# The last block of a large store as fifteen stores of two to fifteen partitions

## The reference

```
keep   = (u >= 0.1)
x_drop = x * keep / 0.9
h      = x + adj @ x_drop
out    = (h - mean(h)) / sqrt(var(h) + 1e-5)      # over the 64 columns of each row
```

## Time and profile before

| what | value |
|---|---|
| median of 3 runs (lowest to highest) | 641.73 us (641.69 to 641.83) |
| the profiled execution's own time | 641.88 us |
| its span, first to last instruction | 640.1 us |
| DMA over the span | 429 GB/s, 274.84 MB |
| TensorE matmul busy | 502.8 us (79%) |
| VectorE, ScalarE busy | 53.7 us, 17.7 us |
| large store (1984 KB), issue and landing | 626.82, 12.7 us later |
| last store (64 KB), issue and landing | 638.09, 1.6 us later |

### The profile page before, as it was taken

The page is one execution under the profiler, slowest core; times in us unless marked ns, Lnnn a source line. Parts: engine busy times, 40 slices in busy tenths (PEclk is TensorE's granted clock), DMA queues, the critical chain, the costliest instruction groups (busy, mean ns, idle before and its releaser), DMA issues.

```text
span 640.1 us, 5097 instructions
## 1 busy us (share of the span) xinstructions
PE 502.8 (79%) x2312; PEld 179.7 (28%) x2312; DVE 53.7 (8%) x102; ACT 17.7 (3%) x41; POOL 1.6 (0%) x14
## 2 busy tenths in 40 slices
PE   0097969688799578879878689867869868689997
PEld 0062213232233222223222223222323223133344
DVE  1930001010010100101000010100101001010101
ACT  0001000000000000000000000000000000000000
POOL 1000000000000000000000000000000000000000
PEclk9997979988799978889979899978999969799999
DMA  9999999999999999999999999999999999999998
GB/s 393 459 394 455 431 420 454 405 446 439 422 421 436 435 451 422 438 408 444 459 418 434 442 412 455 420 434 446 426 418 426 446 451 422 438 405 438 425 425 364
DMA packets 7207, 274.84 MB, mean 429 GB/s; under 512 B 800, under 2 KB 928, under 8 KB 1312
## 3 DMA queue, kind: packets, MB, share of 16 engines
q1 hardware_dynamic: 7056, 272.63, 98.8%
q10 hardware_dynamic: 144, 2.10, 0.8%
HBM read 272.63 MB, written 2.10 MB: 429 GB/s over the span
## 4 chain that ended last, share of the span: by engine, by line
DMA 62%; PE 33%; DVE 3%; another core or an unknown queue 1%; issue 0%; ACT 0%; SPq 0%; DVEq 0%; ACTq 0%
DMA ring<-adj 56%; PE acc L202 33%; DMA ring<-adj_last 5%; DMA xdrop<-u 2%; DVE node_sum L317 1%; DVE xdrop L321 1%; DVE xdrop L329 1%; PE folded L210 0%; DVE x_sb L321 0%; PE lifted L237 0%; SPq L126 0%; ACT squares L303 0%; PE lifted L263 0%; ACT std L308 0%
## 5 line engine op out<-in xcount | busy, mean ns | idle before, releaser
L202 PE MATMUL acc<-ring,xdrop 128*64 128x512 f32 (+1 forms) x2176 | 485.6, 606 | 103.1 <-DMA ring<-adj 101.7
L202 PEld LDWEIGHTS acc<-ring,xdrop 128*64 128x64 f32 x2176 | 162.8, 146 | 413.0 <-issue 280.2
L344 DVE SCALAR_TENSOR_TENSOR y<-folded,x_sb 128x256 f32<-128x256 f32 (+1 forms) x16 | 6.7, 416 | 552.3 <-PE folded L210 552.3
L237 PE MATMUL lifted<-x_sb,lift 128*128 128x64 f32 x4 | 1.1, 428 | 30.6 <-DVE x_sb L321 30.6
L210 PEld LDWEIGHTS folded<-fold,sums_T 128*128 128x128 f32 x128 | 15.5, 191 | 12.6 <-issue 12.6
L284 ACT COPY sums_T<-acc 128x512 f32<-128x512 f32 x15 | 8.8, 585 | 335.0 <-PE acc L202 335.0
L210 PE MATMUL folded<-fold,sums_T 128*128 128x64 f32 x128 | 17.7, 281 | 0.0
L277 ACT ACTIVATE std<-square_sum,eps 128x4 f32<-128x4 f32 (+1 forms) x16 | 4.8, 297 | 225.2 <-DVE square_sum L351 225.2
L237 PEld LDWEIGHTS lifted<-x_sb,lift 128*128 128x128 f32 x4 | 0.9, 322 | 30.5 <-issue 30.5
L348 DVE TENSOR_TENSOR squares<-y 128x256 f32<-128x256 f32 (+1 forms) x16 | 6.7, 417 | 0.5
L355 DVE TENSOR_TENSOR x_sb<-y,rstd 128x256 f32 (+1 forms) x16 | 6.7, 416 | 0.6
(11 more groups left out here) (23 smaller groups left out, 5.5 us busy)
## 6 DMA issues: line engine op xcount, KB each, us to landing
ring<-adj SPq DMA_DIRECT2D x13, 4096.0 KB, 31.3
ring<-adj SPq DMA_DIRECT2D x2, 2048.0 KB, 28.7
xdrop<-u ACTq DMA_DIRECT2D x1, 2048.0 KB, 12.5
x_sb<-x SPq DMA_DIRECT2D x1, 2048.0 KB, 12.3
out<-x_sb SPq DMA_DIRECT2D x1, 1984.0 KB, 12.7
ring<-adj_last SPq DMA_DIRECT2D x1, 1920.0 KB, 29.5
ring<-adj_last SPq DMA_DIRECT2D x1, 1792.0 KB, 33.4
ring<-adj_last SPq DMA_DIRECT2D x1, 1536.0 KB, 30.6
```

The source lines that it names most:

```text
L202: last = nc.tensor.matmul(acc[i][D * h:D * h + D, 0:cols], xdrop[:, k, :], piece[:, b, :], start=(k < 2), stop=(k >= NB - 2))
L344: nc.vector.scalar_tensor_tensor(out=y[:, 0:nj, :], in0=folded[:, 0:nj, :], scalar=1.0 / KEEP, in1=x_sb[:, bass.ds(block0, nj), :], op0=AL ...
```

## The change

The large store goes out with 61 blocks instead of 62. Behind it, with no wait between, SyncE issues 15 stores of the 62nd block: the first 9 partitions, then 15, 14, 13 and so on down to 2, which makes 128. Each has a semaphore of its own, and SyncE waits for each of them after the wait for the other two stores.

```diff
+GROUPS = (9, 15, 14, 13, 12, 11, 10, 9, 8, 7, 6, 5, 4, 3, 2)
...
+        groups = [(sum(GROUPS[:n]), size) for n, size in enumerate(GROUPS)]
...
+        group_stored = [sem(f"group_stored{n}") for n in range(len(groups))]
...
             sp.wait_ge(rows_ready, FINAL)
-            sp.dma_start(out[:, 0:NB - LAST_J, :], x_sb[:, 0:NB - LAST_J, :]).then_inc(stored, 16)
+            bulk = NB - LAST_J - 1
+            sp.dma_start(out[:, 0:bulk, :], x_sb[:, 0:bulk, :]).then_inc(stored, 16)
+
+            for n, (p0, size) in enumerate(groups):
+                sp.dma_start(out[p0:p0 + size, bulk:bulk + 1, :],
+                             x_sb[p0:p0 + size, bulk:bulk + 1, :]).then_inc(group_stored[n], 16)
             sp.wait_ge(rows_ready, FINAL + 1)
             sp.dma_start(out[:, NB - LAST_J:NB, :], x_sb[:, NB - LAST_J:NB, :]).then_inc(stored, 16)
             sp.wait_ge(stored, 32)
+            for n in range(len(groups)):
+                sp.wait_ge(group_stored[n], 16)
```

## The result

The changed kernel takes 644.24 us (median of 6 runs, 644.20 to 644.40) against 641.83 (6 runs, 641.69 to 642.00) of the kernel before: ratio 1.0038, 95% interval 1.0026 to 1.0049. It is slower by 2.4 us, four and a half times the 0.53 that was forecast, and above the range. The profiled execution took 644.23 with a span of 642.4, so the 1.8 around the span is unchanged and the whole difference lies in the span.

A forecast was written before the change was run, and what follows sets the result against it. The DMA stream of adjacency blocks sets the time up to a short tail. Only the waits counted: profiled 641.88 + 0.53 = 642.41, less 0.15 for the median, 642.26, stated as 642.25; range 641.6 to 643.1.

The forecast's parts named there:

- (a): Large store in the tail: losing one block shortens its rows, worth 0 to -0.05 us, taken as 0.
- (b): SyncE's issue of 15 small stores behind the large one: 7.4 us, done at 634.2, covered, no stall.
- (c): Small stores' rows and completions on the DMA rings: delay the last store by 0 to 0.7 us, taken as 0.
- Each completion holds its ring: Rival, DMA rings: each small store's completion blocks its ring 0.4 us, 15 in a row 6.0; time 646 to 648; chance 0.04.
- (d): SyncE's end: 15 more waits, paired into 7 or 8 instructions after the last store's landing, add 0.53 us.
- (e): 15 more semaphores: nothing in the span handles semaphores one by one, so 0.
- SyncE is held in issuing: Rival, SyncE's queue: slow or blocked small-store issues delay the last store; time 646.4 or 647; chance 0.05.
- A low ring is late: Rival, DMA tail: the busiest engine is among the seven late ones, adding 0.1 to 0.7 us; 642.4 to 643.0; chance 0.15.

The follow-up runs named there:

- the small loads: Changed kernel with one semaphore, the large store back at 62 blocks, and 15 same-shaped loads from HBM into spare SBUF replacing the small stores: 644.10 us, +2.28 over the kernel before.

## Why the prediction was wrong

**(a) The shorter large store: right.** It was counted at 0. The last store's packets go out at 638.9 in both kernels.

**(b) The issues: right, and too dear.** 5.45 for fifteen instead of 7.0, since a store of fewer than 16 partitions costs less: 403 ns for the first, 253 for the last, of two partitions. Neither the ring's room nor a count of transfers held SyncE.

**(c) The packets on the rings: this is the step that failed.** It priced a completion as a packet of 25 ns, found up to 0.4 on an evenly filled engine, to be taken by 0.3 of air, and put the term at 0. The packets did just that and were gone by 639.3. But each small transfer takes 0.18 to 0.20 on its ring whatever its packet shows, and the term measured 1.9. The record of increments has it in full. The late sixth ring gets the 11 stores of six partitions or more. Behind a completion of the large store at 639.1 theirs come from 639.28 to 641.287, and the last store's at 641.484: twelve steps of 0.20. With nothing in its way it would have landed 1.6 after its issue, at 639.6.

The rival *Each completion holds its ring* had the mechanism, at a chance of 0.04, with 0.4 a step and 15 steps on a late ring; 0.2 and 10 or 11 were measured. I argued it away with the wrong reading of a right row. The large store lands at 639.5 and the last at 639.7, and I took this 0.2 as proof that nothing stands between completions. It has the size of one step; that it was one is not shown, since the last store's own packets run to 639.3 and its completion comes 0.4 behind them. What the row excluded was 0.4, not 0.2, and the rival should have been priced again at 0.2: 10 to 15 steps of it are 2 to 3. As the reason for the step, the confirmation of writes to HBM, with which the Trainium skill spoke for the rival, is ruled out by the small loads. Its 2.0 for a transfer is given for transfers issued by GpSimd; taken as a step it would be ten times what was measured.

**(d) The waits: near in size by luck, wrong in mechanism.** Forecast 0.53 on the path, since they stand behind `stored` in the code. The build puts the wait for `stored` last, and 15 waits that are satisfied early cost +0.07. In the changed kernel 0.6 is on the path after all, because the small stores land so late that their waits are released late: the last waits take 0.16 of it, and 0.42 is the interval without an instruction, which the prediction did not have. Without the late waits the kernel is 0.2 to 0.4 faster in the medians.

**(e) The semaphores: right**, nothing outside the tail moved.

*SyncE is held in issuing* did not happen. *A low ring is late* came true in part, but not for the busiest ring: in the changed kernel's trace the completions of the large store come early on nine rings (637.3 to 637.8) and late on seven (639.0 to 639.3). The busiest ones, with 15 small stores, are early, and their last small completion comes at 640.0; the sixth and the seventh, with 11 and 10, are late and set the end. Its price of 0.1 to 0.7, made of packets, fell with (c).

The sum as the traces give it: last product 0.09 earlier, landing 1.9 later after its issue, waits and branch 0.6: 2.4, as measured.

## What to carry to other kernels

Count transfers per ring, not bytes and not packets: behind a busy queue each small transfer adds about 0.2 us on every ring that it uses, and a later transfer on that queue lands only after it. Keep small transfers off the queue on whose landing the kernel's end depends; issued early from an idle engine's queue the same fifteen cost nothing that could be measured. And where two landings in a profile lie a small time apart, that time is a candidate for the step, to be multiplied by the number of transfers before a rival is dropped.

## What was not expected of the hardware

A small transfer's step of 0.18 to 0.20 us on a ring does not depend on the direction, on rows of 256 or 512 bytes, or on one or two rows per ring; what it consists of stays open. Packets run ahead of it only in part: rows of a large store behind 15 small ones were held up to 0.9 themselves. Completions on ScalarE's queue did not hold SyncE's loads.

Issuing a transfer of two partitions takes SyncE 253 ns and one of 14 partitions 378, but 15 take 343; one of 16 or 32 takes about 420, hardly less than one of 128 (430, median of L166 in the earlier trace rows). So it is below 16 that the cost falls, if not evenly.

The build reorders consecutive waits on one engine and puts two semaphores into one instruction. In each of these kernels the wait that stands first in the code, for `stored`, came last on the engine. Between the starts of the last of eight wait instructions and of the closing branch lie 0.45 us in both profiles of the changed kernel.
